# The rows of a selective scan: broadcast by TensorE, or through DRAM by DMA

## The reference

```python
dA = dtt[:, :, None] * A                  # (image, channel, state): 256 channels, 16 states
barA = jnp.exp(dA)
inp_term = jnp.einsum('bdn,bn,bd->bn', dA, bt, ut)      # one number per image and state
h = barA * h + inp_term[:, None, :]
y = jnp.einsum('bdn,bn->bd', h, ct) + Dp * ut           # the step's output
```

## Time and profile before

| what | us |
|---|---|
| median of 3 runs (lowest, highest) | 457.06 (456.94, 457.08) |
| the profiled execution, its own time | 456.45 |
| its span, first to last instruction | 454.6 |
| outside the span | 1.85 |
| first scan of state 0 starts | 256.43 |
| last product of the scan ends | 314.37 |
| statistics of y start | 316.35 |

### The profile page before, as it was taken

How to read it: one execution, slowest core, us unless ns; L and a number is a source line. 1 busy time by engine, 2 the same in 40 slices (tenths; PEclk the granted TensorE clock), 3 DMA queues, 4 the chain that set the end, 5 groups by cost and what they waited for, 6 DMA issues and landing times.

```text
span 454.6 us, 8785 instructions
## 1 busy us (share of the span) xinstructions
PE 410.5 (90%) x2944; PEld 325.3 (72%) x2952; DVE 261.3 (57%) x653; ACT 145.7 (32%) x362; POOL 166.6 (37%) x135
## 2 busy tenths in 40 slices
PE   8999999879983999999989876778999899999993
PEld 5675567656773999999956455657667688888872
DVE  1648878866821111112365689998686666565545
ACT  1030077863210112111206685653511123223310
POOL 2008824430173000001460378884000156564560
PEclk9999999999995999999999899999999999999998
DMA  8872194001193468783342000000105567777552
GB/s 274 235 177 80 13 352 149 1 1 56 47 373 111 137 211 294 245 301 130 107 136 72 6 0 0 1 1 1 55 23 153 170 158 181 200 185 189 113 123 101
DMA packets 29884, 58.66 MB, mean 129 GB/s; under 512 B 5806, under 2 KB 19421, under 8 KB 27549
## 3 DMA queue, kind: packets, MB, share of 16 engines
q1 hardware_dynamic: 24189, 46.01, 31.8%
q0 software_dynamic: 5664, 12.25, 10.8%
HBM read 45.66 MB, written 12.59 MB: 128 GB/s over the span
## 4 chain that ended last, share of the span: by engine, by line
PE 62%; DVE 17%; issue 5%; ACT 5%; another core or an unknown queue 3%; DMA 3%; DVEq 1%; SPq 1%; POOL 1%; POOLq 0%; ACTq 0%
PE PS L1877 11%; PE PS L1737 8%; PE PS L1746 7%; PE PS L1892 6%; DVE scratch L1257 4%; PE PS L1958 3%; PE PS L1529 3%; PE PS L1813 2%; PE PS L1692 2%; ACT scratch L708 2%; PE PS L1546 2%; DMA ident<-in_ident 2%; PE PS L1964 2%; DVE xn L904 2%
## 5 line engine op out<-in xcount | busy, mean ns | idle before, releaser
L1877 PE MATMUL PS<-xT,w1s 128*128 128x296 f32 x224 | 60.7, 415 | 0.0
L1877 PEld LDWEIGHTS PS<-xT,w1s 128*128 128x128 f32 x224 | 41.4, 190 | 11.2 <-issue 0.2
L1737 PE MATMUL PS<-scratch,w0up 128*128 128x144 f32 (+1 forms) x256 | 38.2, 310 | 9.2 <-DVE scratch L1167 8.9
L617 POOL DMA_INDIRECT scratch<-xg,idx_nxt x18 | 18.0, 999 | 73.5 <-DVE idx_nxt L1396 39.5
L1257 DVE TENSOR_TENSOR_SCAN scratch<-scratch,PS 128x592 f32<-128x592 f32 x32 | 42.5, 1369 | 4.0 <-PE PS L1820 3.9
L1737 PEld LDWEIGHTS PS<-scratch,w0up 128*128 128x128 f32 x256 | 36.5, 198 | 11.2 <-DVE scratch L1167 9.8
L1184 DVE COPY scratch<-PS 128x144 f32<-128x144 f32 (+1 forms) x16 | 5.1, 320 | 64.4 <-PE PS L1746 64.4
L769 ACT ACTIVATE scratch<-PS 128x288 f32<-128x288 f32 (+1 forms) x32 | 13.8, 431 | 77.0 <-PE PS L1737 77.0
L1892 PE MATMUL PS<-w1s,scratch 128*128 128x256 f32 (+1 forms) x140 | 34.8, 382 | 2.0 <-DVE h L1300 1.1
L1746 PE MATMUL PS<-scratch,w0dn 128*128 128x144 f32 (+1 forms) x256 | 35.2, 296 | 0.0
L1746 PEld LDWEIGHTS PS<-scratch,w0dn 128*128 128x128 f32 x256 | 34.4, 190 | 0.0
(11 more groups left out here) (338 smaller groups left out, 791.1 us busy)
## 6 DMA issues: line engine op xcount, KB each, us to landing
w0dn<-in_w0dn SPq DMA_DIRECT2D x9, 1024.0 KB, 6.0
w0up<-in_w0up SPq DMA_DIRECT2D x9, 1024.0 KB, 6.0
w0dn<-in_w SPq DMA_DIRECT2D x16, 384.0 KB
by_expert<-zeros SPq DMA_DIRECT2D x2, 1920.0 KB, 13.2
w1s<-in_w SPq DMA_DIRECT2D x14, 256.0 KB
w1s<-in_w SPq DMA_DIRECT2D x14, 128.0 KB, 3.3
w0up<-in_patchesT SPq DMA_DIRECT2D x6, 296.0 KB, 4.0
scratch<-by_expert POOLq DMA_DIRECT2D x8, 192.0 KB
```

What stands on the lines that cost most here:

```text
L617: nc.gpsimd.indirect_dma_start(xe1[:, half, q, :], None, xg, bass.IndirectOffsetOnAxis(ap=idx_nxt[:, q:q + 1], axis=0)).then_inc(xe1_in[q] ...
L1737: last = mm(PS[:, z, (f % 2) * width:(f % 2 + 1) * width], w0up[:, s, c, f * P:(f + 1) * P], xeT[:, s, c, 0:width], start=c == 0, stop=c == 1)
L1877: last = mm(PS[:, 2 * n + j, 0:HALF], w1s[:, s, w:w + F1], xT[:, c, half(n)], start=c == 0, stop=c == 1)
```

## The change

Nothing is computed otherwise. The rows reach the partitions in another way, and products are dealt out otherwise.

- The bf16 pieces, their tiles and the selecting matrix `sel` (a load of 384 KB early in the kernel) are gone, with the copies and subtractions that made the pieces, PE's broadcasts of states 2 to 15 and all broadcasts of C, and ACT's copy to cb_sb.
- SP stores the 16 C rows and the 16 input rows to a DRAM tensor rows_bc of 16 x 2 x 592 fp32 numbers. It then loads, for each state from 2 on, both its rows into all 128 partitions with one DMA (592 KB arrive in SBUF), into the tile bcr, four buffers. The C rows of states 0 and 1 come by one DMA of the same size. The load of state n waits until the rows of n - 2 have landed, and until the scans and products of n - 4 are done.
- The two input rows of states 0 and 1 still come through PE, now both ahead of the rest, in banks 3 to 4 and 5 to 6.
- The scans of states 2 to 15 read their second input from bcr in SBUF, not from PSUM.
- BY_POOL becomes all odd states but 15: POOL takes the lower product of seven states, not three.
- The sums of pairs on POOL (7) are gone; PE adds every upper product by itself, so 10 matmuls a state instead of 7.5 on average.

```diff
-        BY_POOL = (3, 7, 11)
+        BY_POOL = (1, 3, 5, 7, 9, 11, 13)
+        def rows_landed(eng, n):
+            eng.wait_ge(bc_in[n % 2 if n >= 2 else 0], 16 * (n // 2 + (n % 2 == 0)) if n >= 2 else 16)
 @block.sync
+            sp.wait_ge(b_c_ready, 2)
+            sp.dma_start(rows_bc[:, 1, :], cT).then_inc(rows_out, 16)
+            sp.wait_ge(rows_out, 16)
+            sp.dma_start(bcr[:, 0:2, 1, :], rows_bc[0:2, 1, :].unsqueeze(0).broadcast_to([P, 2, NT])).then_inc(bc_in[0], 16)
+            sp.wait_ge(inp_ready, 1)
+            sp.dma_start(rows_bc[:, 0, :], inpT).then_inc(rows_out, 16)
+            sp.wait_ge(rows_out, 32)
+            for n in range(2, NS):
+                if n >= BROWS:
+                    rows_landed(sp, n - 2)
+                    sp.wait_ge(scanned, 2 * (n - BROWS) + 2)
+                    low_product(sp, n - BROWS)
+                    sp.wait_ge(hcp_ready, n - BROWS + 1)
+                elif n == 2:
+                    rows_landed(sp, 0)
+                sp.dma_start(bcr[:, n % BROWS, :, :], rows_bc[n].unsqueeze(0).broadcast_to([P, 2, NT])).then_inc(bc_in[n % 2], 16)
 @block.gpsimd
-            for n in range(NS):
-                pool.wait_ge(cb_ready, n + 1)
+            for n in range(NS - 1):
+                rows_landed(pool, n)
                 if n in BY_POOL:
                     pool.wait_ge(scanned, 2 * n + 1)
...
-                if n % 2:
-                    pool.wait_ge(hcp_ready, n + 1)
-                    nc.gpsimd.tensor_tensor(hc[:, 3 + n % 3, :], hc[:, 3 + n % 3, :], hc[:, 3 + (n - 1) % 3, :],
-                                            ALU.add).then_inc(pair_ready, 1)
 @block.scalar
-                act.wait_ge(cb_mm, n + 1)
...
-                nc.scalar.copy(cb_sb[:, n % 2, :], PS[:, 5:7, :].rearrange("p b n -> p (b n)")[:, 0:NT]).then_inc(cb_ready, 1)
 @block.vector
+            def inputs_of(n):
+                if n < 2:
+                    return PS[:, 3 + 2 * n:5 + 2 * n, :].rearrange("p b n -> p (b n)")[:, 0:NT]
+                return bcr[:, n % BROWS, 0, :]
...
-                    nc.vector.tensor_tensor_scan(hs[:, n % 2, c, :], barA[:, k % BA, :], IB, 0.0, ALU.mult, ALU.add).then_inc(scanned, 1)
+                    nc.vector.tensor_tensor_scan(hs[:, n % 2, c, :], barA[:, k % BA, :], inputs_of(n), 0.0, ALU.mult, ALU.add).then_inc(scanned, 1)
...
-            dve.wait_ge(pair_ready, NS // 2 - 1)
+            dve.wait_ge(upper_used, NS - 3)
 @block.tensor
             for n in range(NS):
-                broadcast(3, inp3, n, ib_mm)
-                broadcast(5, c3, n, cb_mm)
+                add_products(n)
```

More of the change, by code:

```diff
@@ L231, in vit_tower @@
         RING = 6
-        (u, dt, dtu, spa, spb, bT, cT, inpT, rest, barA, hs, hc, du) = views(
+        BROWS = 4
+        (u, dt, dtu, spa, spb, bT, cT, inpT, barA, hs, hc, du, bcr) = views(
             (P, (2, NT)), (P, (2, NT)), (P, (2, NT)), (P, (2, NT)), (P, (2, NT)),
[L234 to L238, removed]
+            (NS, (NT,)), (NS, (NT,)), (NS, (NT,)),
+            (P, (BA, NT)), (P, (2, 2, NT)), (P, (RING, NT)), (P, (2, NT)), (P, (BROWS, 2, NT)))
+        rows_bc = nc.dram_tensor("rows_bc", (NS, 2, NT), F32, kind="Internal").ap()
         a_neg = sb("a_neg", [P, 2, NS])
@@ L324, in vit_tower @@
         bc_mm, b_c_ready = sem("bc_mm"), sem("b_c_ready")
-        c_part, c_rest, inp_part, inp_rest = (sem(n) for n in ("c_part", "c_rest", "inp_part", "inp_rest"))
+        rows_out, bc_in = sem("rows_out"), [sem(f"bc_in{q}") for q in range(2)]
         sp_taken_max = sem("sp_taken_max")
@@ L330, in vit_tower @@
         g_mm, inp_ready, du_ready = sem("g_mm"), sem("inp_ready"), sem("du_ready")
-        barA_ready, ib_mm, cb_mm, scanned = sem("barA_ready"), sem("ib_mm"), sem("cb_mm"), sem("scanned")
-        cb_ready, hcp_ready, pair_ready, pair_used = (sem(n) for n in ("cb_ready", "hcp_ready", "pair_ready", "pair_used"))
+        barA_ready, ib_mm, scanned = sem("barA_ready"), sem("ib_mm"), sem("scanned")
+        hcp_ready, upper_used = (sem(n) for n in ("hcp_ready", "upper_used"))
         hcg_ready = sem("hcg_ready")
@@ L399, in _ @@
                               (b_dt[:, :], "b_dt"), (a_log[:, :, :], "a_log"), (d_p[:, :], "d_p"),
-                              (sel[:, :, :], "sel"), (w_inT[:, :, :], "w_inT"), (sel_f[:, :, :], "sel_f")):
+                              (w_inT[:, :, :], "w_inT"), (sel_f[:, :, :], "sel_f")):
                 sp.dma_start(dst, A[name]).then_inc(scan_in, 16)
@@ L596, in _ @@
                 pool.wait_ge(scanned, 2 * n + 2)
-                if n == NS - 1:
-                    break
                 if n >= 3:
-                    if n % 2:
[L601 to L604, removed]
+                    pool.wait_ge(upper_used, n - 2)
+                nc.gpsimd.tensor_tensor(hc[:, 3 + n % 3, :], hs[:, n % 2, 1, :], bcr[:, n % BROWS, 1, :],
@@ L1246, in _ @@
                                     bT.rearrange("p (b n) -> p b n", b=2), ALU.mult).then_inc(inp_ready, 1)
-            IB = PS[:, 3:5, :].rearrange("p b n -> p (b n)")[:, 0:NT]
+            def inputs_of(n):
+                if n < 2:
+                    return PS[:, 3 + 2 * n:5 + 2 * n, :].rearrange("p b n -> p (b n)")[:, 0:NT]
+                return bcr[:, n % BROWS, 0, :]
             for n in range(NS):
-                dve.wait_ge(ib_mm, n + 1)
+                if n < 2:
+                    dve.wait_ge(ib_mm, n + 1)
+                else:
+                    rows_landed(dve, n)
                 for c in range(2):
@@ L1636, in _ @@
             keep_busy(7, 4)
[L1637 removed]
+            pe.wait_ge(scan_in, 8 * 16)
             scan_low_weights()
@@ L1815, in add_to_y, with broadcast @@
                 return last
-            def broadcast(bank, row, n, done, row_of=sel):
-                mm(PS[:, bank, 0:512], row_of[:, n, :], row[:, 0:512], start=True, stop=True)
-                mm(PS[:, bank + 1, 0:NT - 512], row_of[:, n, :], row[:, 512:NT], start=True, stop=True).then_inc(done, 1)
+            def broadcast(bank, row, n, done):
+                mm(PS[:, bank, 0:512], sel_f[:, n, :], row[:, 0:512], start=True, stop=True)
+                mm(PS[:, bank + 1, 0:NT - 512], sel_f[:, n, :], row[:, 512:NT], start=True, stop=True).then_inc(done, 1)
             def add_products(n):
@@ L1824, in add_products @@
                 add_to_y(hc[:, n % 3, :], 0).then_inc(hc_used, 1)
-                if n % 2:
-                    pe.wait_ge(pair_ready, (n + 1) // 2)
-                    add_to_y(hc[:, 3 + n % 3, :], 1).then_inc(pair_used, 1)
-            for n in range(NS):
[L1830 to L1840, removed]
-                    broadcast(3, inp3, n, ib_mm)
[L1842 to L1845, removed]
-                broadcast(5, c3, n, cb_mm)
[L1847 to L1857, removed]
+                if n < NS - 1:
+                    pe.wait_ge(hcp_ready, n + 1)
+                    add_to_y(hc[:, 3 + n % 3, :], 1).then_inc(upper_used, 1)
+            pe.wait_ge(inp_ready, 1)
+            pe.wait_ge(b_c_ready, 2)
+            for n in range(2):
+                broadcast(3 + 2 * n, inpT, n, ib_mm)
+            start_y()
+            pe.wait_ge(du_ready, 1)
+            for c in range(2):
+                add_to_y(du[:, c, :], c)
+            for n in range(NS):
+                add_products(n)
             for bank in range(3):
@@ L2053, in shape_constants @@
                 maskb=np.ascontiguousarray(np.broadcast_to(np.where(ok, 0.0, MASKED).astype(f)[:, None, :], (GR, 4, GR))).astype(bf),
-                ropet=ropet, ropeq=ropet * np.float32(SCALE), sel=sel, sel_f=sel_f,
+                ropet=ropet, ropeq=ropet * np.float32(SCALE), sel_f=sel_f,
                 before=np.ascontiguousarray(before))
```

50 lines of the change are left out of this document (7 added, 43 removed).

## The result

The change is slower: a median of 470.63 us (469.6 to 471.29, 4 runs) against 457.0 (456.5 to 457.08, 4 runs), a ratio of 1.0314 with a 95% interval of 1.0286 to 1.0342. The forecast was 475.3 with 466 to 483. The profiled execution took 471.23 us with a span of 469.5; it is the one that the sum is held against.

The account below looks back on a forecast made before the run. DVE was taken to set the scan's pace, POOL close behind. Serialised work +18.9, tail -1.2 and handing over +0.5 gave +18.2 on 456.45, 474.7; with 0.6 to the median, 475.3 us, range 466 to 483.

Parts of the forecast that it names:

- the sum: Scan, states 2 to 15: DVE's and POOL's work one after the other, last product ending at 333.3 against 314.37, +18.9 us.
- The second input: Scans from state 2 on, both inputs in SBUF: they and POOL's products run one after the other; chance 0.77.
- The rival in which scans let POOL through: Scans at half throughput let POOL go between, so DVE alone sets the pace: 8.7 us faster, 448.4; chance 0.12.
- What a turn costs: POOL in states 2 to 15: 19 products at 1.42 us each, 27.0 us, added to DVE's time.
- DVE's 42.3: DVE in states 2 to 15: 28 scans 36.1, products 5.4, last upper product in halves 0.83.
- its term for handing over: Switches between DVE and POOL: from 1.9 us less to 3.0 more, taken as +0.5.
- The start: Stores and loads up to state 2: it starts at 263.0, not 267.16, a gain of 4.2 us.
- the 1.0 for them: POOL's three products of states 0 and 1 end at 264.0, 1.0 us after state 2 could start.
- The tail: After the last product: statistics start 0.8 us later, not 1.98, a gain of 1.2.
- The clock: PE's clock might fall, costing only the tail: taken as 0, with +3 us kept for the range.
- The loads as the bound: Rival: loads read by 128 partitions take 7.4 us a state, 51 us later, 508 in all; chance 0.06.
- The signs named ahead: POOL's products or scans at 2.7 us, two states in about 10.1, waits alternating DVE and POOL, state 2 near 263.

Follow-up runs that it names:

- e1: The changed kernel with scans of states 2 to 15 reading their second input from PSUM (wrong rows): stage 50.50 us, against 74.14 in the change.
- e6: The kernel before with scans of states 2 to 15 reading their second input from SBUF: stage 87.02 us, ratio 1.0639 to the kernel before.
- e4: Own version: input rows through PSUM by PE, C rows by DMA, no pair sums, odd lower products on POOL: ratio 0.9829 to the kernel before, stage 51.38 us.
- e8: The version with input rows by PE and C by DMA, plus lower products of states 2, 6 and 10 on POOL: ratio 0.978 to the kernel before.
- e3: The changed kernel with all products on DVE and none on POOL: stage 64.25 us, ratio 1.0107 to the kernel before.
- e2: The changed kernel with all lower products on DVE, upper ones still on POOL: stage 71.79 us, ratio 1.025 to the kernel before.
- e5: The changed kernel without the loads of states 4 to 15 (wrong rows): stage 74.27 us, ratio 1.0327 to the kernel before.
- e7: The changed kernel with the store of the input rows ahead of the first load of C rows: stage 74.99 us, against 74.14 in the change.

## Why the prediction was right

The mechanism was right, its size 4.0 us too large over the stage. Both are counted from the start of the first scan, which by itself came 0.65 us later than in the trace of before, through nothing that the change touches in the scan.

- **The second input.** That a scan with two SBUF inputs would take turns with POOL was read off the collisions of DVE's product and confirmed by e1 and e6 from both sides. The rival in which scans let POOL through is refuted by e6 and by the single scans above.
- **What a turn costs, the term that was mis-sized.** The sum charged DVE 1.42 for each of POOL's 19 products, its whole record. From state 2's start to the end of the last product are 330.06 - 264.67 = 65.4 us; less DVE's 42.3 leaves 23.1, or 1.21 a product. So part of POOL's 1.43, some 0.2, lies beside DVE's instruction. The rows had half of it: POOL's product ended 1.32 after DVE's and not 1.43, which the prediction used only as the lower end of its term for handing over, against a guess of +3.0 for the upper one. That is -3.9, and the +0.5 for handing over was nothing. (Six lower products of these states on POOL and not three is right; that of state 3, which the text under the listings counts as leaving DVE, was on POOL before.)
- **The start.** State 2 was to start 6.6 us after scan 0 and starts 7.59 after it. The loads went as reckoned (4.1 for 592 KB, 4.2 forecast; 1.6 for the first store, 1.8 forecast), but the store of the inputs took 4.9 us beside the load and not 3.8: +1.0. In return POOL's products of state 1 ended at 264.72, just as state 2 started, so the 1.0 for them fell away.
- **The tail.** 1.16 us from the last product to the statistics, 0.8 forecast and 1.98 before: +0.4.
- **The clock.** It did fall: the mean from 280 to 329 is 0.86. Why stays open: it is 1.00 in the same stage of e4 and e8, where PE is busy nearly all the time, but also in e3 from 260 to 306, where PE is busy for 29.2 of 46 us, and here for 32.7 of 49. In the change DVE waited for PE only in the tail, and the stretch from 330 to 335 is at 1.00. The part behind the statistics takes 138.3 us in both kernels. The +3 kept for it was not needed; that the clock can fall in the tail is seen in e2, at a cost of 0.3.
- **The loads as the bound.** Refuted by e5.
- **The signs named ahead.** They came, each a little smaller or later: POOL's products at 2.38 to 2.51 us and scans at 2.55 to 2.65 (2.7 forecast), two states in 9.47 (10.1), state 2 at 264.67 (263). The chain of waits showed nothing either way.

Together 1.0 - 1.0 - 3.9 - 0.5 + 0.4 = -4.0, and +0.65 for the start of the scan: 474.7 becomes 471.35. The profiled execution took 471.23; the last 0.1 lies outside the span (1.73 us, not 1.85).

The rule of the Trainium skill that was cited (page "SBUF — State Buffer", section "Who interferes with whom") holds for scans too: with two inputs in SBUF 2.55 beside a product of POOL, 1.38 without one; with one input in PSUM 1.35 to 1.39 in the kernel before and in e1, beside products or not. The prediction took from it that the port is held for a whole instruction; the runs show a hold of 1.21 for a recorded 1.43. The half throughput of the scan, from the Trainium skill's page "DVE: opcode table, instruction layouts, handler registers and perf-mode slots" (section "Datapath and trigger behaviour"), did not let POOL through.

## What to carry to other kernels

Before moving an operand from PSUM to SBUF, ask what else runs on POOL: here, with fp32 rows of 128x592, a DVE scan or product with two SBUF inputs and a POOL product took turns, and a scan with an input in PSUM did not disturb POOL. Where they add up, a product is better left on DVE (0.67) than given to POOL (1.21 of DVE's time, 1.43 of its own); where they don't, giving it away is a gain of its whole length. A DVE at 100% in a table of busy times may be waiting for half of many an instruction: compare the mean duration of a line with its minimum before calling the engine full.

## What the runs showed of the hardware that was not expected

- The hold is shorter than the record: POOL's product of 1.43 us holds a scan up by 1.21.
- A store of 37 KB landed in 1.6 us with no load of rows beside it (the first store), the second store in 3.5 with a load of 592 KB issued 0.35 us behind it (e7), and in 4.9 with one issued 0.7 us ahead of it. What it waits for is open.
- A load in which all 128 partitions read the same 4.7 KB of DRAM is not slow: 3.4 to 5.2 us for 592 KB, 3.8 in the median, where 256 KB took 2.8 and 1024 KB 6.0, 4.2 if one goes evenly between them.
- Two chips differ by 12 us in the kernel before (444.81 and 456.75), and about 10 of them lie ahead of the scan: it starts at 246.4 in e6 and at 256.4 in the trace of before.
